# Two graph layers on one core: the second layer's adjacency tiles from a transposed input on GpSimd's queue, in place of a stored copy turned by DMA

## Chip, core and metric

The kernel runs on one core of one Trainium2 chip. The metric is the device time of one execution in microseconds (us), the median over the runs. Three runs of the kernel before gave 2017.46, 2017.54 and 2022.37 us.

## What is computed

```python
def layer0(query, key, value, adj, Wq, bq, Wk, bk, Wv, bv, Wm, bm):
    q, k, v = query @ Wq.T + bq, key @ Wk.T + bk, value @ Wv.T + bv
    scores = (q @ k.T) / 4096 ** 0.5 * adj
    scores = where(abs(scores) < 1e-05, -1e9, scores)
    return softmax(scores) @ v @ Wm.T + bm
def layer1(features, adj, W, b):
    return relu(adj @ features @ W.T + b)
x = layernorm(x + layer0(x, key, value, adj, ...))
x = layernorm(x + layer1(x, adj, W, b))
```

x, key and value are 4096 x 512 and adj is 4096 x 4096, all float32 in device memory; adj holds zeros and ones. The output is 4096 x 512.

## The kernel before

**Layer 0.** Rows are taken in 32 tiles of 128 (NT = 32). The keys are cut in two halves, and each half is a pass over all 32 row tiles, so there are 64 units, numbered 0 to 63. For a unit TensorE makes the scores (`scores`, line 934), VectorE masks them with a half row block of the adjacency (`adjh`, two buffers, loaded by GpSimd's queue in `load_adj`, line 771, with float32 turned into bf16 on the way), ScalarE makes exponentials, both split the probabilities into an fp16 high and low part (`Phl`), SyncE's queue turns these by DMA transposes (`turn_prob`: `PT<-Phl`, lines 423 and 426), and TensorE weighs the values with them (`weigh`, line 954). In the second pass the merged result is split (`Uhl`), turned (`turn_merged`, lines 552 and 555), multiplied by the joined weights (`project`, line 975) and normalised; this is a row tile of x1. It is split, turned (`turn_x1`, lines 539 and 542, into the single buffer `x1T`, only after the tile before it has been multiplied) and multiplied by W (`rows_product`, line 989): a tile of Y. Each operand is held as high and low part, and a product of two is 48 or 12 matmuls of 512 columns. In the second pass TensorE goes round: scores of unit g, rows_product, weigh of unit g - 1, project of unit g - 2.

**Layer 1.** With W applied first, what is left is adj @ Y. `AT[h][k]` are four SBUF buffers of 1 MB, each one row tile of the adjacency turned. Output tiles come in pairs p = 0 to 15, tile p and tile p + 16. Pairs 0 and 1 are plain products (`aggregate`, line 1061, 64 matmuls a tile). Pairs 2 to 15 (`seven`, line 1094) use seven products of 16 matmuls in place of eight blocks: VectorE makes four sums of adjacency blocks for the next pair (`adj_sum`, line 2153) and combines the results (`pair`, lines 2160 and 2165), adds bias and x1, and normalises (lines 2108 to 2124). For the last pair `last_pair` (line 2214) does it in halves of 256 columns.

**Where the adjacency tiles come from.** In every unit SyncE's queue stores the half row block that GpSimd's queue has loaded (`store_adj`, `adj_bf<-adjh`, line 410) as bf16 in device memory. Pairs 0 and 1 are turned from there in quarters (`adj_part`, line 560) between the other work of SyncE's queue at the end of layer 0: six quarters before the last unit's probabilities, two after x1 tile 29, four after the last merged tile, and four at the end. From pair 2 on whole tiles are turned (`adj_tile`, line 566), as soon as six of the seven products of pair p - 2 are made. Each queue works in its written order, and a wait holds everything written behind it.

**The order at the end of layer 0.** Y is in memory by now but for its last tiles. GpSimd's queue loads it in seven groups of four tiles, 1 MB each (`load_y`, line 794): groups 0 and 1 early, 4, 5 and 6 once the last probabilities are turned, 2 and 3 once x1 tile 30 is turned; then the signed sums (`load_sums`, 5.5 MB in all). TensorE's order is:

```
weigh(63); rows_product(28); project(62)
aggregate(0,0, m 0-8); rows_product(29); aggregate(0,0, 16-20); project(63)
aggregate(0,0, 20-28); aggregate(0,1, 0-8); rows_product(30)
aggregate(0,1, 16-28); aggregate(1,0, 0-8); rows_product(31)
aggregate(0,k, 8-16), the last four m of both, the rest of pair 1; seven() for pairs 2 to 15
```

## Time and profile before

| | us |
|---|---|
| median of three runs | 2017.54 |
| the profiled execution | 2020.34 |
| its span, first to last instruction | 2018.7 |
| TensorE busy | 1999.7 |
| VectorE busy | 1461.4 |
| ScalarE busy | 687.0 |

The stages by TensorE's work: weights, queries and keys to about 120 us, the first pass to 825, the second to 1598, the change to layer 1 to 1672, the fourteen pairs of seven products to 2010, and then the last tile's end. A row of a timeline gives start and duration in us, engine, line, operation and count; in brackets stands the idle time before it and what ended that. Matmuls overlap: a row's duration is longer than its pace, which is 216 ns a matmul everywhere (10.36 us for 48). PEclk is 1.00 where TensorE is granted its full 2.4 GHz. Times to landing are counted from the issue of a DMA to its semaphore.

### The profile page before, as it was taken

How to read it: one execution, taken by the hardware profiler on the slowest of the kernel's cores; microseconds unless marked ns; L12 is line 12 of the kernel's file. 1: busy time of each engine (PE TensorE's matmuls, PEld its weight loads, DVE VectorE, ACT ScalarE, POOL GpSimd, SP SyncE). 2: the span in 40 equal slices, each digit the busy share in tenths (PEclk: the TensorE clock that was granted, in tenths of full speed). 3: DMA queues.
4: the chain of work that ended last, by engine and by line, in shares of the span. 5: the costliest groups of instructions: out<-in, count | busy, mean ns of one | idle time of the engine just before them, and what ended most of it. 6: DMA issues, size and time to landing. Idle time of an engine off the chain costs nothing.

```text
span 2018.7 us, 29119 instructions
## 1 busy us (share of the span) xinstructions
PE 1999.7 (99%) x9243; PEld 915.3 (45%) x9243; DVE 1461.4 (72%) x3380; ACT 687.0 (34%) x853; POOL 95.3 (5%) x141
## 2 busy tenths in 40 slices
PE   8999999999999999999999999999999999999998
PEld 5444444444444444444444444444444444444443
DVE  7875666656666666777777777788888668788887
ACT  6853433334343443433333333344343210000000
POOL 5000000000000000000000000000000000000000
PEclk9999999999999999999999999999999999999999
DMA  7667777667777777777666667777777996555551
GB/s 284 242 172 171 189 186 201 155 155 161 188 171 181 179 170 215 180 165 167 166 166 162 162 165 165 165 166 182 180 184 206 223 277 141 125 130 137 130 134 62
DMA packets 564919, 351.22 MB, mean 174 GB/s; under 512 B 482176, under 2 KB 486272, under 8 KB 562944
## 3 DMA queue, kind: packets, MB, share of 16 engines
q1 hardware_dynamic: 547072, 279.26, 54.9%
q0 software_dynamic: 17792, 71.31, 15.4%
q8 instruction: 25, 0.41, 0.1%
q14 instruction: 30, 0.25, 0.0%
HBM read 176.95 MB, written 88.60 MB: 132 GB/s over the span
## 4 chain that ended last, share of the span: by engine, by line
PE 98%; SPq 1%; DVE 1%; DMA 0%; issue 0%; ACT 0%; DVEq 0%
PE ps L954 33%; PE ps L934 33%; PE ps L1094 17%; PE ps L905 4%; PE ps L989 4%; PE ps L975 4%; PE ps L1061 2%; SPq L560 1%; PE ps L853 0%; PE ps L848 0%; DMA x1T<-x1hl 0%; DMA wb<-in_Wk 0%; PE ps L835 0%; PE ps L866 0%; DVE weighed L1480 0%
## 5 line engine op out<-in xcount | busy, mean ns | idle before, releaser
L954 PE MATMUL ps<-V,PT 128*128 128x512 f16 x3072 | 673.3, 379 | 1.0 <-issue 1.0
L934 PE MATMUL ps<-KT,thl 128*128 128x512 f16 x3072 | 673.2, 379 | 0.0
L954 PEld LDWEIGHTS ps<-V,PT 128*128 128x128 f16 x3072 | 300.5, 98 | 363.7 <-issue 2.0
L934 PEld LDWEIGHTS ps<-KT,thl 128*128 128x128 f16 x3072 | 300.6, 98 | 362.2
L1718 DVE SCALAR_TENSOR_TENSOR prob<-ps,c_now,adjh 128x512 f32<-128x512 f32 x256 | 191.8, 750 | 262.3 <-PE ps L934 261.2
L1273 ACT ACTIVATE small<-prob 128x512 f32<-128x512 f32 x256 | 161.1, 630 | 619.3 <-DVE prob L1718 334.0
L1747 DVE SCALAR_TENSOR_TENSOR Phl<-prob,Phl 128x2048 f16<-128x2048 f32 x64 | 146.6, 2291 | 73.8 <-ACT Phl L1286 73.6
L1731 DVE CUSTOM_DVE_ANT_0 prob<-prob,small 128x512 f32<-128x512 f32 x256 | 174.4, 683 | 0.0
L1278 ACT ACTIVATE prob<-prob,nbias,inv 128x2048 f32<-128x2048 f32 x64 | 134.0, 2094 | 99.6 <-DVE nbias L1740 99.6
L1724 DVE TENSOR_SCALAR small<-small,eps_s,neg_s 128x512 f32<-128x512 f32 x256 | 138.9, 542 | 21.0 <-ACT small L1273 21.0
L1286 ACT ACTIVATE Phl<-prob 128x2048 f16<-128x2048 f32 x64 | 122.3, 1910 | 7.1
L1449 ACT ACTIVATE p<-ps 128x512 f32<-128x512 f32 x14 | 8.4, 597 | 323.5 <-PE ps L1094 323.5
L776 POOL DMA_DIRECT2D adjh<-in_adj x64 | 35.8, 559 | 1365.6 <-DMA adj_bf<-adjh 725.1
L1094 PE MATMUL ps<-Y,AT 128*128 128x512 f16 x448 | 99.0, 379 | 0.0
L975 PE MATMUL ps<-Wvm,UT 128*128 128x512 f16 x384 | 88.1, 379 | 2.5 <-DMA UT<-Uhl 2.5
L989 PE MATMUL ps<-W1T,x1T 128*128 128x512 f16 x384 | 88.1, 379 | 0.1
L905 PE MATMUL ps<-xT,Aq 128*128 128x512 f16 x384 | 84.5, 379 | 0.4 <-DVE xT L1558 0.4
L1094 PE MATMUL ps<-Ta,S 128*128 128x512 f16 x336 | 79.4, 379 | 0.0
L1094 PE MATMUL ps<-Tb,S 128*128 128x512 f16 x336 | 79.4, 379 | 0.0
L1094 PEld LDWEIGHTS ps<-Y,AT 128*128 128x128 bf16 x448 | 43.8, 98 | 52.9
L975 PEld LDWEIGHTS ps<-Wvm,UT 128*128 128x128 f16 x384 | 37.5, 98 | 48.0 <-DMA UT<-Uhl 3.0
L989 PEld LDWEIGHTS ps<-W1T,x1T 128*128 128x128 f16 x384 | 37.5, 98 | 45.7 <-DMA x1T<-x1hl 0.6
(208 smaller groups left out, 1695.1 us busy)
## 6 DMA issues: line engine op xcount, KB each, us to landing
adjh<-in_adj POOLq DMA_DIRECT2D x64, 512.0 KB, 5.4
adj_bf<-adjh SPq DMA_DIRECT2D x64, 512.0 KB, 4.6
t_in<-t_dram SPq DMA_DIRECT2D x64, 256.0 KB, 3.2
x_in<-in_x SPq DMA_DIRECT2D x64, 256.0 KB, 4.5
xraw<-in_x_t SPq DMA_DIRECT2D x8, 1024.0 KB, 8.6
t_dram<-tq POOLq DMA_DIRECT2D x8, 1024.0 KB, 5.8
o_dram<-z_out SPq DMA_DIRECT2D x32, 256.0 KB, 2.8
o_in<-o_dram SPq DMA_DIRECT2D x32, 256.0 KB, 4.6
```

Source lines behind the costliest of these rows:

```text
L905: last = nc.tensor.matmul(ps[:, BT + e, :], Aq[:, m, k, e * P:(e + 1) * P], xT[:, b, s, k, :], start=(n == 0), stop=(n == 3 * KD - 1))
L934: last = nc.tensor.matmul(ps[:, BS + c, :], thl[:, b, s, k * P:(k + 1) * P], KT[:, m, k, c * C:(c + 1) * C], start=(n == 0), stop=(n == 3 ...
L954: last = nc.tensor.matmul(ps[:, BU + b, :], PT[:, b, s, m, :], V[:, v, m, :], start=(m == 0 and q == 0), stop=(m == MT - 1 and q == 2))
L975: last = nc.tensor.matmul(ps[:, BZ, :], UT[:, b, s, k, :], Wvm[:, m, k, :], start=(n == 0), stop=(n == 3 * KD - 1))
L989: last = nc.tensor.matmul(ps[:, BY, :].rearrange("p (o n) -> p o n", n=P), x1T[:, s, k, :], W1T[:, m, :, k, :], start=(q == 0), stop=(q == ...
L1094: last = nc.tensor.matmul(ps[:, bank, :].rearrange("p (s d) -> p s d", s=2), left(m), right(m), start=(m == 0), stop=(m == NP - 1))
L1273: nc.scalar.activation(small[:, c % 2, :], prob[:, b, c * C:(c + 1) * C], ACT.Abs).then_inc(s_abs, 1)
L1278: nc.scalar.activation(prob[:, b, :], prob[:, b, :], ACT.Exp, bias=nbias[:, b:b + 1], scale=inv[:, half:half + 1], accum_out=rsum[:, b:b + ...
L1718: nc.vector.scalar_tensor_tensor(out=prob[:, b, c * C:(c + 1) * C], in0=ps[:, BS + c, :], scalar=c_now[:, b:b + 1], in1=adjh[:, b, c * C:( ...
L1724: nc.vector.tensor_scalar(small[:, c % 2, :], small[:, c % 2, :], eps_s[:, half:half + 1], neg_s[:, half:half + 1], ALU.is_lt, ALU.mult).t ...
L1731: nc.vector.tensor_tensor_reduce(out=prob[:, b, c * C:(c + 1) * C], in0=prob[:, b, c * C:(c + 1) * C], in1=small[:, c % 2, :], scale=1.0, ...
L1747: nc.vector.scalar_tensor_tensor(out=Phl[:, b, LO, :], in0=prob[:, b, :], scalar=P_SCALE, in1=Phl[:, b, HI, :], op0=ALU.mult, op1=ALU.subt ...
```

## The change

The host hands over a second form of the adjacency, `adj_t`, float32, in which each row tile is already laid out turned: `adj_t[t, p, m, n]` is `adj[128 t + n, 128 m + p]`. GpSimd's queue loads a tile of it straight into its buffer, with float32 turned into bf16 on the way (`load_tile`, 2 MB read and 1 MB written). `store_adj`, `adj_part`, `adj_tile` and the copy `adj_bf` are gone; `turned_used` keeps the wait that `store_adj` had. Tiles 0 and 16 are loaded in the middle of the second pass, so their buffers have moved to where the first half's keys were, and eight tiles of Y have moved to the probabilities' place (`Yfront`, read through `y_tiles`); groups 0 and 1 of Y are loaded later for that. TensorE's order at the end of layer 0 differs, and the last pair's end is written anew: the upper tile's right half is scaled in two steps straight from PSUM, and the lower tile's last step is on ScalarE. In the diff, waits for `16 * PARTS` quarters, which become waits for 16, and places where `Y[:, n]` became `y_tiles(n, 1)` are left out, as are declarations.

```diff
@@ -165,13 +165,15 @@
         with ExitStack() as second:
-            Y = sb(second, "Y", [P, NT, 2, D], fp16)
+            AT00 = sb(second, "AT00", [P, NT, P], bf16)
+            AT01 = sb(second, "AT01", [P, NT, P], bf16)
+            Y = sb(second, "Y", [P, NT - FRONT, 2, D], fp16)
             Ta = sb(second, "Ta", [P, PT2, 4, 2, H], fp16)
-            AT00 = sb(second, "AT00", [P, NT, P], bf16)
+            Yfront = sb(second, "Yfront", [P, FRONT, 2, D], fp16)
             AT10 = sb(second, "AT10", [P, NT, P], bf16)
-            AT01 = sb(second, "AT01", [P, NT, P], bf16)
             AT11 = sb(second, "AT11", [P, NT, P], bf16)
             with ExitStack() as signs:
                 Yr = sb(signs, "Yr", [P, 2, 2, D], fp32)
...
@@ -186,6 +188,9 @@
             Tb = sb(second, "Tb", [P, PT2, 4, 2, H], fp16)
             S34 = sb(second, "S34", [P, 2, HALF], bf16)
         AT = ((AT00, AT01), (AT10, AT11))
+        def y_tiles(n, count):
+            return Yfront[:, n:n + count, :, :] if n < FRONT else Y[:, n - FRONT:n - FRONT + count, :, :]
...
@@ -363,6 +368,10 @@
         def place(p, k):
             return 2 * p + (k if p < PLAIN else 1 - k)
+        LOWER_READY = (ROOT_STEPS + 3) * 2 * (NP - 1) + 8 + 2 + 2 * ROOT_STEPS - 2 + 1
...
@@ -403,12 +412,9 @@
                     wait(sp, s_z, n - 1)
                     load_x(n, b)
-                def store_adj(g, n, b, j, half):
+                def turned_used(g):
                     wait(sp, o_mm, g - 1)
-                    sp.wait_ge(adj_in[b], 16 * (j + 1))
-                    sp.dma_start(adj_bf[bass.ds(n * P, P), half * HALF:(half + 1) * HALF], adjh[:, b, :])\
-                      .then_inc(ab_st[b], 16)
...
@@ -455,9 +461,11 @@
                     nb, nj = 1 - b, j + b
                     load_t(g + 2, (g + 2) % NT if isinstance(g, int) else g + 2)
+                    if not isinstance(g, int):
+                        sp.to_reg(g - 1)
                     wait(sp, s_c, g)
+                    turned_used(g)
                     load_x(g + 1, nb)
-                    store_adj(g, g, b, j, 0)
                     if chunk is not None:
                         load_chunk(2 * chunk + b, b, chunk)
                     turn_prob(g, b)
...
@@ -554,17 +562,6 @@
                     sp.wait_ge(u_lo, g - NT + 1)
                     sp.dma_start_transpose(UT[:, b, LO, :, :], Uhl[:, LO, :]).then_inc(ul_in[b], 16)
-                def adj_part(p, k, part):
-                    t, w = p + NP * k, N // PARTS
-                    sp.dma_start_transpose(AT[p][k][:, part * (NT // PARTS):(part + 1) * (NT // PARTS), :],
-                                           adj_bf[t * P:(t + 1) * P, part * w:(part + 1) * w]).then_inc(at_in[p][k], 16)
-                def adj_tile(p, k):
-                    t = p + NP * k
-                    sp.dma_start_transpose(AT[p % 2][k][:, :, :], adj_bf[t * P:(t + 1) * P, :]).then_inc(at_in[p % 2][k], 16)
...
@@ -592,18 +591,6 @@
                         if isinstance(n, int) and n == NT - NP + TC:
                             sp.wait_ge(yf_st, 16 * NP)
                         load_copy(n - NP - TC, b)
-                    if isinstance(n, int) and n == NT - 1:
-                        for k in range(2):
-                            sp.wait_ge(ab_st[k], 16 * (NT // 2 + NP // 2 + 1))
-                        sp.wait_ge(p_lo, g)
-                        for part in range(PARTS):
-                            adj_part(0, 0, part)
-                        sp.wait_ge(ph_in[0], 16 * NT)
-                        sp.wait_ge(pl_in[0], 16 * NT)
-                        for part in range(2):
-                            adj_part(0, 1, part)
                     turn_prob(g, b)
...
@@ -654,22 +641,13 @@
                 last = 2 * NT - 1
                 turn_x1(NT - 3)
                 store_x1(NT - 3, 1)
-                for part in range(2, PARTS):
-                    adj_part(0, 1, part)
                 turn_merged(last, 1)
-                sp.wait_ge(p_lo, 2 * NT)
-                for part in range(PARTS):
-                    adj_part(1, 0, part)
                 turn_x1(NT - 2)
                 store_x1(NT - 2, 0)
                 sp.wait_ge(y_st, 16 * (NT - TC))
                 sp.dma_start(b1_rep[:, :], b1.rearrange("(a n) -> a n", a=1).to_broadcast([P, D])).then_inc(s_bm, 16)
                 turn_x1(NT - 1)
                 store_x1(NT - 1, 1)
-                sp.wait_ge(ph_in[1], 16 * NT)
-                sp.wait_ge(pl_in[1], 16 * NT)
-                for part in range(PARTS):
-                    adj_part(1, 1, part)
...
@@ -679,28 +657,20 @@
                     sp.dma_start(zf[:, k, :], x1_dram[t * P:(t + 1) * P, :]).then_inc(zf_in[k], 16)
                 for b in range(2):
-                    sp.wait_ge(ab_st[b], 16 * NT)
                     sp.wait_ge(o_st[b], 16 * NT)
                 for k in range(2):
                     load_row(0, k)
-                for p in range(NP):
-                    if p + 2 < NP:
-                        q = p - PLAIN
-                        if q < 0:
-                            sp.wait_ge(f_mm, 2 * (p + 1))
-                        else:
-                            sp.wait_ge(s_prod, 7 * q + 6)
-                            sp.wait_ge(s_comb, 4 * (q + 1))
-                        for k in range(2):
-                            adj_tile(p + 2, k)
-                    if p + 1 < NP:
-                        for k in range(2):
-                            load_row(p + 1, k)
+                for p in range(1, NP):
+                    for k in range(2):
+                        load_row(p, k)
                 for k in (1, 0):
                     t = NP - 1 + NP * k
-                    sp.wait_ge(f_res, place(NP - 1, k) + 1)
+                    if k == 1:
+                        sp.wait_ge(s_lower, 1)
+                    else:
+                        sp.wait_ge(f_res, place(NP - 1, k))
                     sp.dma_start(out[t * P:(t + 1) * P, :], y[:, k, :]).then_inc(last_st, 16)
                 sp.wait_ge(last_st, 32)
                 for k in range(2):
...
@@ -772,7 +742,6 @@
                     if not isinstance(g, int) or g >= 2:
                         pool.wait_ge(s_adj, MC * (g - 1))
-                        pool.wait_ge(ab_st[b], 8 * (g - b))
                     pool.dma_start(adjh[:, b, :], adj[bass.ds(n * P, P), half * HALF:(half + 1) * HALF])\
                         .then_inc(adj_in[b], 16)
...
@@ -785,13 +754,28 @@
                 with pool.Fori(1, NT // 2) as i:
                     for b in range(2):
                         load_adj(2 * i + b, b, 2 * i + b, 0)
-                with pool.Fori(0, NT // 2) as i:
+                def load_tile(p, k):
+                    t = p + NP * k
+                    pool.dma_start(AT[p % 2][k][:, :, :], adj_t[t, :, :, :]).then_inc(at_in[p % 2][k], 16)
+                SECOND = (NP + TC) // 2
+                with pool.Fori(0, SECOND) as i:
                     for b in range(2):
                         load_adj(2 * i + b, b, NT + 2 * i + b, 1)
+                pool.wait_ge(w_turned, 32)
+                for k in range(2):
+                    load_tile(0, k)
+                    load_adj(2 * SECOND + k, k, NT + 2 * SECOND + k, 1)
+                with pool.Fori(SECOND + 1, NT // 2) as i:
+                    for b in range(2):
+                        load_adj(2 * i + b, b, NT + 2 * i + b, 1)
                 def load_y(c):
                     pool.wait_ge(y_st, 16 * TC * (c + 1))
-                    pool.dma_start(Y[:, c * TC:(c + 1) * TC, :, :],
+                    pool.dma_start(y_tiles(c * TC, TC),
                                    y_dram[c * TC:(c + 1) * TC, :, :, :].rearrange("t p s d -> p t s d")).then_inc(y_ld[c][0], 16)
...
-                pool.wait_ge(w_turned, 32)
-                for c in (0, 1):
-                    load_y(c)
+                pool.wait_ge(p_lo, 2 * NT - 1)
+                load_y(0)
                 pool.wait_ge(pl_in[1], 16 * NT)
+                load_y(1)
                 for c in (4, 5, 6):
                     load_y(c)
+                pool.wait_ge(ph_in[0], 16 * NT)
+                pool.wait_ge(pl_in[0], 16 * NT)
+                load_tile(1, 0)
                 pool.wait_ge(ts_st, 16 * EARLY)
                 pool.wait_ge(x1t_in, 32 * (NT - 1))
                 for c in (2, 3):
                     load_y(c)
+                pool.wait_ge(ph_in[1], 16 * NT)
+                load_tile(1, 1)
                 pool.wait_ge(x1t_in, 32 * NT)
                 for c in range(2):
                     load_sums(c, Ta[:, 4 * c:4 * c + 4, :, :, :])
                 pool.wait_ge(y_mm, NT)
                 load_sums(2, Tb[:, 0:EARLY - 8, :, :, :])
-                for k in range(2):
-                    store(0, k)
-                for p in range(1, NP - 1):
+                for p in range(NP - 1):
+                    if p + 2 < NP:
+                        q = p - PLAIN
+                        if q < 0:
+                            pool.wait_ge(f_mm, 2 * (p + 1))
+                        else:
+                            pool.wait_ge(s_prod, 7 * q + 6)
+                            pool.wait_ge(s_comb, 4 * (q + 1))
+                        for k in range(2):
+                            load_tile(p + 2, k)
                     for k in range(2) if p < PLAIN else (1, 0):
                         store(p, k)
...
@@ -1058,26 +1057,26 @@
                             elif m % TC == 0:
                                 pe.wait_ge(*y_ld[m // TC])
                         for s in (HI, LO):
...
+                pe.wait_ge(s_adj, MC * 2 * NT)
+                aggregate(0, 0, 0, 4)
                 project(2 * NT - 2, 0, NT - 1)
-                pe.wait_ge(s_adj, MC * 2 * NT)
-                aggregate(0, 0, 0, 8)
+                aggregate(0, 0, 4, 8)
                 rows_product(NT - 3)
-                aggregate(0, 0, NP, NP + 4)
+                aggregate(0, 1, 0, 8)
                 project(2 * NT - 1, 1, NT - 1)
-                aggregate(0, 0, NP + 4, NT - TC)
-                aggregate(0, 1, 0, 8)
+                aggregate(0, 0, NP, NT - TC)
                 rows_product(NT - 2)
                 aggregate(0, 1, NP, NT - TC)
+                rows_product(NT - 1)
                 aggregate(1, 0, 0, 8)
-                rows_product(NT - 1)
                 for k in range(2):
                     aggregate(0, k, 8, NP)
...
@@ -1452,6 +1451,9 @@
                     copy_first_product(q)
                 with act.Fori(2, NP - PLAIN) as q:
                     copy_first_product(q)
+                act.wait_ge(f_step, LOWER_READY)
+                nc.scalar.activation(y[:, 1, :], y[:, 1, :], ACT.Identity, bias=ra2[:, 1:2], scale=rstd2[:, 1:2]).then_inc(s_lower, 1)
             @block.vector
...
@@ -2256,33 +2266,42 @@
                     taken(q, 3, u2[:, :], p1[:, :], ps[:, 3, :], ALU.add)
                     dve.wait_ge(c_step, 11 * q + 3)
                     taken(q, 4, u5[:, :], u2[:, :], ps[:, 2, :], ALU.add)
+                    dve.wait_ge(c_step, 11 * q + 4)
+                    nc.vector.tensor_tensor(cs[:, 0, H:D], u5[:, 0:H], u5[:, H:D], ALU.add).then_inc(c_step, 1)
                     dve.wait_ge(s_prod, 7 * q + 5)
-                    dve.wait_ge(c_step, 11 * q + 4)
-                    taken(q, 5, csum[:, 1, :], u5[:, :], ps[:, 6, :], ALU.add)
-                    together(q, 5, 1, 1, 1)
-                    taken(q, 7, u3[:, :], u2[:, :], ps[:, 6, :], ALU.add)
-                    half(1, 1, bst2, 6)
+                    taken(q, 6, csum[:, 1, :], u5[:, :], ps[:, 6, :], ALU.add)
+                    together(q, 6, 1, 1, 1)
+                    taken(q, 8, u3[:, :], u2[:, :], ps[:, 6, :], ALU.add)
+                    half(1, 1, bst2, 7)
+                    scaled(0, 1, cs[:, 0, H:D], b1_rep[:, H:D])
                     dve.wait_ge(s_prod, 7 * q + 6)
-                    dve.wait_ge(c_step, 11 * q + 7)
-                    taken(q, 8, csum[:, 0, :], u3[:, :], ps[:, 5, :], ALU.subtract)
-                    together(q, 8, 0, 1, 0)
-                    half(1, 0, bst2, 9)
+                    dve.wait_ge(c_step, 11 * q + 8)
+                    taken(q, 9, csum[:, 0, :], u3[:, :], ps[:, 5, :], ALU.subtract)
+                    together(q, 9, 0, 1, 0)
+                    half(1, 0, bst2, 10)
                     begin(1, bst2)
                     for step in range(2):
                         root_step(1, step, 0)
                     dve.wait_ge(s_prod, 7 * q + 7)
-                    taken(q, 10, csum[:, 1, :], u5[:, :], ps[:, 4, :], ALU.add)
-                    together(q, 10, 1, 0, 1)
-                    half(0, 1, bst, 11)
+                    for s in range(2):
+                        dve.wait_ge(f_out, done[0])
+                        scaled(0, 1, ps[:, 4, s * H:(s + 1) * H], y[:, 0, H:D])
+                    deviation(0, 1, bst)
                     begin(0, bst)
                     for step in range(ROOT_STEPS - 2):
                         root_step(1, step + 2, 1)
                         root_step(0, step, 1)
                     dve.wait_ge(f_step, steps[0] - 1)
-                    finish(1)
-                    for step in range(ROOT_STEPS - 2, ROOT_STEPS):
-                        root_step(0, step, 0)
+                    nc.vector.scalar_tensor_tensor(out=ra2[:, 1:2], in0=mv2[:, 1, 0:1], scalar=-1.0, in1=rstd2[:, 1:2],
+                                                   op0=ALU.mult, op1=ALU.mult).then_inc(f_step, 1)
+                    steps[0] += 1
+                    assert steps[0] == LOWER_READY
+                    root_step(0, ROOT_STEPS - 2, 1)
+                    root_step(0, ROOT_STEPS - 1, 0)
                     dve.wait_ge(f_step, steps[0])
                     finish(0)
...
@@ -2301,7 +2320,7 @@
     x, key = inputs["x"], inputs["L0_gnn_key"]
     half = key.shape[0] // 2
-    laid_out = [("x", x), ("x_t", blocks(x, 512)), ("adj", inputs["adj"]),
+    laid_out = [("x", x), ("x_t", blocks(x, 512)), ("adj", inputs["adj"]), ("adj_t", blocks(inputs["adj"], 128)),
                 ("key_t0", blocks(key[:half], 512)), ("key_t1", blocks(key[half:], 128))]
     for name in ("value", "Wq", "Wk", "Wv"):
         laid_out.append((name, inputs["L0_gnn_" + name]))
```

## Rows read from the trace of the kernel before

**Rows 1.** Page, part 1: busy us and share of the span.

```profile
PE 1999.7 (99%) x9243; PEld 915.3 (45%) x9243; DVE 1461.4 (72%) x3380; ACT 687.0 (34%) x853; POOL 95.3 (5%) x141
```

**Rows 2.** Windows: stretch, us, busy of each engine, PEclk, DMA share, GB/s.

```profile
200.00:400.00 200.00, 200.00 (x929) 90.78 (x928) 133.26 (x266) 76.45 (x88) 5.33 (x10) 1.00 0.76 183
...
1840.00:1864.00 24.00, 24.00 (x113) 10.88 (x112) 19.53 (x44) 0.60 (x1) 1.08 (x2) 1.00 0.52 131
```

**Rows 3.** Timeline of TensorE at the end of layer 0.

```profile
1587.67 10.52 PE L954 MATMUL ps<-V,PT 128*128 128x512 f16 x48 [0.51 <-issue]
...
1603.28 2.75 PE L975 MATMUL ps<-Wvm,UT 128*128 128x512 f16 x12 [2.50 <-DMA UT<-Uhl]
...
1616.22 7.07 PE L1061 MATMUL ps<-Y,AT 128*128 128x512 f16 x32
1623.41 2.76 PE L989 MATMUL ps<-W1T,x1T 128*128 128x512 f16 x12
...
1634.64 2.75 PE L989 MATMUL ps<-W1T,x1T 128*128 128x512 f16 x12
```

**Rows 4.** Timeline of SyncE's queue in the same stretch.

```profile
1569.63 9.14 SPq L560 DMA_TRANSPOSE AT<-adj_bf  x6
...
1583.27 1.35 SPq L426 DMA_TRANSPOSE PT<-Phl  x1
...
1590.98 2.05 SPq L552 DMA_TRANSPOSE UT<-Uhl  x1
...
1626.26 1.26 SPq L539 DMA_TRANSPOSE x1T<-x1hl  x1
```

**Rows 5.** DMA from 1588 to 1600: queue, packets, MB, share; then issues, us to landing.

```profile
q0 software_dynamic: 506, 1.98, 61.6%
q1 hardware_dynamic: 1209, 0.97, 41.9%
...
UT<-Uhl SPq DMA_TRANSPOSE x2, 10.9
```

**Rows 6.** DMA from 1626 to 1630; no other queue has a row there.

```profile
q0 software_dynamic: 351, 1.37, 92.1%
...
x1T<-x1hl SPq DMA_TRANSPOSE x2, 6.5
```

**Rows 7.** DMA from 1636 to 1650.

```profile
q0 software_dynamic: 397, 5.53, 94.7%
q1 hardware_dynamic: 809, 0.20, 8.2%
```

**Rows 8.** DMA from 1314 to 1322: one load of adjh.

```profile
q0 software_dynamic: 144, 0.52, 41.3%
```

**Rows 9.** DMA view of the whole run: issues, median us to landing.

```profile
UT<-Uhl SPq DMA_TRANSPOSE x64, 2.5
```

**Rows 10.** Timelines of VectorE around x1 tile 30, and of POOL.

```profile
1610.95 0.69 DVE L1851 SCALAR_TENSOR_TENSOR x1hl<-z_out,x1hl 128x512 f16<-128x512 f32 x1 [0.70 <-ACT x1hl L1338]
...
1587.97 1.49 POOL L794 DMA_DIRECT2D Y<-y_dram  x2 [63.80 <-DMA PT<-Phl]
```

**Rows 11.** Timelines of SyncE's queue and VectorE in one pair of seven products.

```profile
1837.72 9.41 SPq L566 DMA_TRANSPOSE AT<-adj_bf  x2
...
1853.34 1.22 DVE L2153 TENSOR_TENSOR S<-AT 128x2048 bf16<-128x2048 bf16 x1
```

**Rows 12.** Timeline of VectorE at the end.

```profile
2007.00 0.69 DVE L2160 TENSOR_TENSOR csum<-u,ps 128x512 f32<-128x512 f32 x1 [0.37 <-PE ps L1094]
...
2010.39 0.69 DVE L2160 TENSOR_TENSOR csum<-u,ps 128x512 f32<-128x512 f32 x1
...
2011.58 0.48 DVE L2223 SCALAR_TENSOR_TENSOR y<-cs,inv_y,b_rep 128x256 f32<-128x256 f32 x1
2012.17 0.42 DVE L2228 SCALAR_TENSOR_TENSOR y<-y,zf 128x256 f32<-128x256 f32 x1
...
2014.76 0.54 DVE L2247 TENSOR_SCALAR y<-y,mv,rstd 128x512 f32<-128x512 f32 x1
```

47 lines of the change are left out of this document (27 added, 20 removed).

## The prediction

> **What bounds the kernel now.** I read the page's busy times first, then the windows, then the timelines of TensorE and of SyncE's queue at the end of layer 0, the DMA view by short stretches, and the end. TensorE is busy for 1999.7 of 2018.7 us [rows 1], and in the passes without a break and at the full clock [rows 2]. The change leaves every matmul in place, so only TensorE's idle time can move. Of that some 7 us lie before 100 us, where nothing changes. Three gaps lie at the end of layer 0: 0.51 us before weigh(63), 2.50 us before project(62), which waits for the turned merged tile, and 0.3 us before rows_product(30) [rows 3] (its row starts at 1623.41, while 32 matmuls of 216 ns from 1616.22 end at 1623.13). The rest is the end after the last matmul, from 2010.39 on [rows 12].
>
> The sum is made on the profiled execution, 2020.34 us, which is 2.8 us above the median of the runs, 2017.54. I take the same difference off the median.
>
> **The passes: 0.** 64 stores of the half row block leave SyncE's queue, and DMA traffic falls. TensorE waits for none of it [rows 2], so this buys nothing. `turned_used` keeps the wait. The first two tiles are loaded in the second pass on GpSimd's queue, each ahead of one load of adjh. One load of adjh keeps the 16 DMA engines for 41.3% of 8 us = 3.3 us [rows 8]. A tile is twice the bytes, so 6.6 us. The load of adjh behind it is issued when unit g - 2 is masked, some 40 us ahead of its own masking, and the transposes of the unit have over 10 us to spare before TensorE wants them. Cost 0; if that cover were gone, 6.6 us twice.
>
> **The pairs of seven products: 0.** SyncE's two transposes took 9.4 us to issue, from 1837.72, and VectorE took the first sum from the tiles at 1853.34 [rows 11], 15.6 us later. After the change two loads of 6.6 us each and about 2 us to start and land make 15.2 us. VectorE is busy for 19.53 of 24 us [rows 2], so a few us more are made up within the pair, and TensorE wants that sum only some 17 us after it is made (it serves the third product of the next pair). The two zf loads and the two stores of a pair (1 MB) fit beside 13.2 us in 24.2. Two stores now stand behind two loads on GpSimd's queue; they are issued 7 and 14 us later, when their data are made, and nobody waits for them for some 10 us. Cost 0.
>
> **The end of layer 0.** This is where the change decides. SyncE's queue loses sixteen quarter transposes; six ran just before the last probabilities were turned [rows 4]. GpSimd's queue gains: group 1 of Y moves behind the last probabilities, next to groups 4, 5 and 6, and a tile follows at once. Before, groups 4 and 5 stood there alone, issued at 1587.97 [rows 10]. So after 1588 there are 4 MB of Y and a tile of 6.6 us in one unbroken row on that queue, where there were 2 MB, a pause, and 1 MB.
>
> *What such a load does to a transpose.* A transpose of a merged or x1 tile lands 2.5 us after issue in calm [rows 9]. With two groups of Y under way it took 10.9 [rows 5]. From 1626 to 1630, with x1T issued at 1626.26 [rows 4], GpSimd's queue moved 351 packets and the hardware queue none, and x1T landed after 6.5 us, about 1.3 us after the last packets of the load [rows 6]. From 1636 to 1650 the hardware queue moved 809 packets in 14 us, 58 a us, beside 5.53 MB [rows 7]. So the transposes advance hardly or slowly as long as GpSimd's queue has work.
>
> By the Trainium skill ("DMA: Bandwidth & Descriptors", Queues, rings and completion order) an engine takes turns between its queues, packet by packet. This trace agrees from 1636 to 1650 at most and not from 1626 to 1630, where a queue that had been issued to got no turn.
>
> *The gap of 0.51.* It ends as the last low transpose, issued at 1583.27 [rows 4], lands 4.3 us later. Without the quarters ahead of the pair [rows 4] I put its issue where VectorE has made its data, at about 1582.8, and its landing at 1587.1. **-0.5.**
>
> *project(62).* TensorE now comes to it at 1587.16 + 10.36 + 2.59 + 8 x 0.216 = 1601.8. SyncE issues the merged tile's two transposes at about 1589.0 and 1590.3, 2 us earlier than before, as nothing stands in its way; GpSimd's data start at about 1589.5. Y drains at 1.37 MB in 4 us = 0.34 MB a us [rows 6]: 4 MB take 11.8 us, and with the tile the queue is empty at 1607.9. If the transposes slip in ahead they land by 1601.8 and TensorE waits for nothing; if they wait for all of it, at 1609.4, a gap of 7.6. At 58 packets a us [rows 7] their some 1,000 packets take 17.7 us, to 1608. Part of the first gets through before the load is at full strength, so I take 1606, a gap of 4.2 where there were 2.5: **+1.7**. rows_product(29) is then reached at 1606 + 2.6 + 1.7 = 1610.3, and x1T of tile 29, issued at 1600.2, lands at about 1609.4 with the queue: no further gap.
>
> *project(63), rows_product(30).* SyncE's queue has no quarters now between the x1 and merged transposes. x1T of tile 30 needs 5.8 us from the end of project(62) (1605.86 to 1611.64 [rows 10]), and TensorE has 11.2 us of other work between rows_product(29) and (30). **-0.3**, the small gap.
>
> *rows_product(31).* It now comes 5.2 us after rows_product(30), where it came 8.6 us after it [rows 3]. Its transposes can't be issued before rows_product(30) ends, because `x1T` is single. GpSimd's queue begins groups 2 and 3 and then tile (1,1) when x1T of tile 30 has landed, and I put that 8 us after rows_product(29) starts. Then come 2 us to start, 2 MB at 0.34 = 5.9, and 6.6 for the tile: free at 22.5, x1T landed at 23.8, while TensorE comes at 21.6. Gap 2.2. At the 0.395 MB a us of [rows 7], with the tile's 2 MB read at that pace too, it is 0. I take the middle: **+1.1**.
>
> Tiles for pairs 2 and 3 are issued as pairs 0 and 1 end, behind 5.5 MB of signed sums; at 0.395 these are over by about 1655, and two tiles by about 1668, before 1671.9 when pair 2 starts. **0.** The sums of VectorE start with rows_product(31) and have 3.4 us more to spare than before.
>
> **The end.** Before, 2010.39 to 2012.17 goes for a sum of 512 columns, a join and a scaling [rows 12]. Two scalings of 256 columns, 0.59 from one to the next as in the last two of these rows, take 1.2: -0.6. One more such scaling stands before the last product, in a stretch with 0.37 us to spare: +0.15. The lower tile's last step, 0.54 between the root steps, goes to ScalarE for one of 0.2: -0.3. Its store goes ahead of the last one as before. Together **-0.8**, between -0.9 and 0.
>
> **Sum:** -0.5 + 1.7 - 0.3 + 1.1 - 0.8 = +1.2, so 2021.5 for such an execution and **2018.7** as the median.
>
> **Rivals.**
> *A, the queue of loads holds TensorE up (slower).* The transposes for project(62) and for rows_product(31) wait for all that is ahead on GpSimd's queue. At 0.34 MB a us the gaps are 7.6 and 2.2: -0.5 + 5.1 - 0.3 + 2.2 - 0.8 = +5.7. At the pace of 1.98 MB in some 9 us [rows 5], 0.22, Y takes 18.2 us, the merged tile lands at 1615.8, gap 14.0, and the second is some 5: +14.9. The middle, **2027**. It is past the bound of slower once the merged tile lands after 1609.9. For it: rows 5 and 6. Against it: the two transposes are issued 2 us sooner.
> *B, the transposes slip through.* No gap is left: -3.3 - 0.8 = -4.1, **2013.4**. By the skill's turns the merged tile gets every second packet; at the 58 a us that the trace shows beside a load that is 1608, not in time, so the rule alone doesn't make this case. It needs the head start or shorter loads.
> *C, the pairs become bound by their loads.* Were two tiles to take over 24.2 us instead of 15.2, each of 14 pairs would stretch; at 27 us that is +39, **2057**. Against it: 3.3 us for half a tile [rows 8].
> *D, the copy's removal frees TensorE in the passes.* Against it: no gap there [rows 2].
>
> **How the numbers follow.** Forecast 0.42, A 0.25, B 0.25, C 0.02, and 0.06 for a gain past every term (D, or a run-to-run difference). A measurement of this kernel can tell about 0.3%, 6 us. The forecast and B are within it: same 0.67. Slower is A and C, 0.27; faster 0.06. The range takes in B whole and A to its middle: 2013.0 to 2027.5.
>
> **What would show it.** Right: TensorE's timeline has no gap before weigh(63), one of 2 to 6 us before project(62) ended by UT<-Uhl, none before rows_product(30), a short one before rows_product(31); VectorE takes a pair's first sum within 3 us of the time before, and TensorE has no gap from pair 2 on; the span ends 7.5 us after the last product instead of 8.3. Wrong: transposes with landings of 2.5 us amid the loads (B), hardware packets near none until 1610 or later (A), or VectorE waiting for AT in every pair (C).

## The result, and the profile after

Nine executions of the changed kernel have a median of 2027.95 us (2026.45 to 2036.92), nine of the kernel before 2018.74 us. The ratio is 1.0054, with a 95% interval of 1.0044 to 1.0064. So the change is slower, by 9.2 us in the medians, where 2018.7 us was forecast and the range ended at 2027.5. That is the place where rival A stood (2027). Six of the nine took 2026.45 to 2029.01 us and three 2033.31 to 2036.92.

The profiled execution took 2026.45 us (span 2024.8) and is the fastest of the nine. Beside that of before (2020.34, span 2018.7) it is 6.1 us longer. First the page's busy times, after:

```profile
PE 2000.0 (99%) x9243; PEld 914.9 (45%) x9243; DVE 1461.3 (72%) x3381; ACT 687.6 (34%) x854; POOL 116.3 (6%) x173
```

Against [rows 1] TensorE has the same work, 9243 matmuls, and GpSimd has 32 instructions more. What differs is idle time of TensorE and one stretch at half its clock, worked out below. Windows of the kernel after (stretch, us, busy of each engine, PEclk, DMA share, GB/s): a piece of the first pass, six pieces at the end of layer 0, and the pairs of seven products.

```profile
200.00:400.00 200.00, 200.00 (x928) 90.77 (x927) 133.77 (x268) 77.02 (x88) 5.40 (x10) 1.00 0.68 157
...
1599.00:1607.00 8.00, 6.44 (x30) 2.57 (x27) 3.53 (x7) 1.11 (x2) 0.26 (x1) 1.00 1.12 292
1607.00:1609.00 2.00, 0.00 (x0) 0.00 (x0) 1.68 (x10) 0.00 (x0) 0.00 (x0) 1.00 1.14 219
1609.00:1611.00 2.00, 0.00 (x0) 0.00 (x0) 0.45 (x1) 0.00 (x0) 0.00 (x0) 0.65 0.93 191
1611.00:1613.00 2.00, 0.00 (x0) 0.00 (x0) 0.00 (x0) 0.00 (x0) 0.00 (x0) 0.50 1.25 136
1613.00:1615.00 2.00, 1.55 (x4) 0.59 (x5) 0.69 (x1) 0.63 (x1) 0.00 (x0) 0.50 0.80 211
1615.00:1617.00 2.00, 2.00 (x7) 0.77 (x6) 0.00 (x0) 0.00 (x0) 0.00 (x0) 0.64 0.00 0
```

```profile
1672.00:1990.00 318.00, 318.00 (x1475) 144.16 (x1474) 256.42 (x560) 7.76 (x13) 29.08 (x53) 1.00 0.56 130
```

These pieces of the passes and of the pairs have no gap, and from 300 to 825 us TensorE is busy for 524.87 of 525 us; DMA traffic in the first pass fell from 183 [rows 2] to 157 GB/s and bought nothing. Between 1607 and 1613.45 us TensorE does nothing, and in that pause the granted clock falls to 0.50, the lower level of 1.2 GHz, and returns to 1.00 only after 1615.

TensorE's timeline after, the rows that answer to [rows 3]:

```profile
1586.13 10.52 PE L953 MATMUL ps<-V,PT 128*128 128x512 f16 x48 [0.32 <-issue]
...
1602.47 2.75 PE L974 MATMUL ps<-Wvm,UT 128*128 128x512 f16 x12 [1.51 <-DMA UT<-Uhl]
1605.06 1.89 PE L1060 MATMUL ps<-Yfront,AT 128*128 128x512 f16 x8
1613.45 4.23 PE L988 MATMUL ps<-W1T,x1T 128*128 128x512 f16 x12 [6.50 <-DMA x1T<-x1hl]
...
1620.97 2.75 PE L974 MATMUL ps<-Wvm,UT 128*128 128x512 f16 x12
...
1637.70 2.76 PE L988 MATMUL ps<-W1T,x1T 128*128 128x512 f16 x12 [1.03 <-DMA x1T<-x1hl]
```

A row of TensorE names what a wait ended with; `rows_product` multiplies a turned tile of x1 (`x1T`), `project` a turned merged tile (`UT`). The large gap, 6.50 us, stands before rows_product(29), where I forecast none, and the wait is for x1T of tile 29. The 28 matmuls from 1613.45 to 1620.97 take 7.52 us, where 28 x 0.216 is 6.05: the low clock costs 1.47 us more. Against the kernel before: -0.19 before weigh(63), -0.99 before project(62), +6.50 and +1.47 here, -0.28 before rows_product(30), +1.03 before rows_product(31). That is +7.5.

To compare executions without the scatter of the kernel's beginning I measure a **stretch**: from where TensorE is done before weigh(63) (its start less its gap) to the start of the last product's 16 matmuls. Before it is 2006.74 - 1587.16 = 419.58, after 2013.26 - 1585.81 = 427.45, so +7.87: the gaps and the clock, to within 0.3 us.

Now GpSimd's and SyncE's queues after:

```profile
1586.43 0.76 POOL L778 DMA_DIRECT2D Yfront<-y_dram  x1 [29.27 <-DMA PT<-Phl]
1587.18 1.49 POOL L778 DMA_DIRECT2D Y<-y_dram  x2
1597.96 0.75 POOL L778 DMA_DIRECT2D Y<-y_dram  x1 [9.29 <-DMA y_dram<-Yst]
1598.70 0.57 POOL L761 DMA_DIRECT2D AT<-in_adj_t  x1
...
1623.51 0.57 POOL L761 DMA_DIRECT2D AT<-in_adj_t  x1
```

```profile
1591.63 3.69 SPq L563 DMA_TRANSPOSE UT<-Uhl  x1
...
1599.33 1.21 SPq L547 DMA_TRANSPOSE x1T<-x1hl  x1
1600.63 1.21 SPq L550 DMA_TRANSPOSE x1T<-x1hl  x1
1601.89 0.57 SPq L538 DMA_DIRECT2D x_dram<-z_out  x1
1602.70 7.08 SPq L560 DMA_TRANSPOSE UT<-Uhl  x1
```

Groups 1, 4 and 5 of Y go out together, but group 6 waits 9.29 us for the store of its tiles and goes out at 1597.96, with the tile (1,0) behind it at 1598.70. In this pause the merged tile's transposes get through, and project(62) starts at 1602.47. Group 6's own data come late: from 1601 to 1603 GpSimd's queue moved 5 packets, from 1603 to 1606 282. The two transposes of x1 tile 29 are issued 0.6 and 1.9 us after the tile's load; the first lands after 13.7 us, the second at about 1613.3. One more transpose behind them even takes 7.08 us to be issued.

The DMA queues from 1606 to 1608 and from 1608 to 1610 (queue, packets, MB, share of 16 engines):

```profile
q0 software_dynamic: 45, 0.36, 94.4%
q1 hardware_dynamic: 45, 0.01, 7.3%
...
q0 software_dynamic: 48, 0.39, 93.6%
q1 hardware_dynamic: 49, 0.01, 4.7%
```

GpSimd's queue moved 45 packets and SyncE's 45, then 48 and 49. So here the two queues advance one for one, but a packet of the tile's load is 8 KB and one of a transpose 0.25 KB. It isn't so wherever a load and a transpose meet. The transposes of x1 tile 31 were issued at 1631.58 and 1632.87, beside tile (1,1), and from 1632 to 1634 the hardware queue has no row at all:

```profile
q0 software_dynamic: 53, 0.43, 104.7%
```

From 1612 to 1614, with the load of tile (1,0) over, the hardware queue moved 1073 packets:

```profile
q1 hardware_dynamic: 1073, 0.48, 96.5%
```

**The end.** VectorE's timeline, the rows that answer to [rows 12], then ScalarE's step for the lower tile and the two stores on SyncE's queue:

```profile
2016.92 1.00 DVE L2223 SCALAR_TENSOR_TENSOR y<-ps,inv_y,y 128x256 f32<-128x256 f32 x2
2018.03 0.43 DVE L2238 SCALAR_TENSOR_TENSOR y<-y,zf 128x256 f32<-128x256 f32 x1
...
2021.19 0.55 DVE L2257 TENSOR_SCALAR y<-y,mv,rstd 128x512 f32<-128x512 f32 x1
...
2020.81 0.81 ACT L1456 ACTIVATE y<-y,ra,rstd 128x512 f32<-128x512 f32 x1 [23.92 <-DVE ra L2298]
...
2021.65 0.82 SPq L674 DMA_DIRECT2D out<-y  x2
```

From the last product's 16 matmuls to the end of the span it is 11.54 us, where it was 11.96: -0.42.

### The profile page after: what moved, and what is told of

It reads as the page before. It is cut to its first block, busy times and chain, and to the rows that moved or that the text cites. A ratio compares the mean times of both kernels' runs of the same rounds, so it can differ in the third digit from the quotient of the medians.

```text
span 2024.8 us, 28869 instructions
## 1 busy us (share of the span) xinstructions
PE 2000.0 (99%) x9243; PEld 914.9 (45%) x9243; DVE 1461.3 (72%) x3381; ACT 687.6 (34%) x854; POOL 116.3 (6%) x173
## 4 chain that ended last, share of the span: by engine, by line
PE 98%; DMA 1%; DVE 1%; SPq 0%; ACT 0%; issue 0%; DVEq 0%
PE ps L953 33%; PE ps L933 33%; PE ps L1093 17%; PE ps L988 4%; PE ps L904 4%; PE ps L974 4%; PE ps L1060 2%; DMA x1T<-x1hl 1%; PE ps L852 0%; PE ps L847 0%; DVE weighed L1482 0%; DVE Aq L1601 0%; DMA wb<-in_Wk 0%; PE ps L834 0%; DVE mcol L1588 0%; DVE xT L1560 0%
## 5 line engine op out<-in xcount | busy, mean ns | idle before, releaser
L1093 PE MATMUL ps<-Y,AT 128*128 128x512 f16 x336 | 74.8, 379 | 0.0
L904 PEld LDWEIGHTS ps<-xT,Aq 128*128 128x128 f16 x384 | 37.5, 98 | 45.6 <-DVE xT L1560 1.4
```

The source lines that it names most:

```text
L904: last = nc.tensor.matmul(ps[:, BT + e, :], Aq[:, m, k, e * P:(e + 1) * P], xT[:, b, s, k, :], start=(n == 0), stop=(n == 3 * KD - 1))
L1093: last = nc.tensor.matmul(ps[:, bank, :].rearrange("p (s d) -> p s d", s=2), left(m), right(m), start=(m == 0), stop=(m == NP - 1))
```

## The experiments

Each kernel was timed in three rounds beside the kernel before on the same chip (the last one in five). The ratio and its interval are those given for these runs side by side; it isn't the quotient of the two medians and can differ from it by 0.2%. Gaps and stretch are from the profiled execution; the first two gaps stand before weigh(63) and project(62), where nothing else is named, and "half clock" means that the group behind a gap took over 4 us for 12 matmuls instead of 2.75, or over 12.9 for 48 instead of 10.52.

| kernel | median, before | ratio, 95% interval | stretch | gaps of TensorE at the end of layer 0, us |
|---|---|---|---|---|
| before | | | 419.58 | 0.51; project(62) 2.50; rows_product(30) 0.28 |
| after | 2027.95, 2018.74 | 1.0054 (1.0044 to 1.0064) | 427.45 | 0.32; 1.51; rows_product(29) 6.50, half clock; (31) 1.03 |
| e1 | 2026.67, 2018.81 | 1.0030 (1.0014 to 1.0045) | 426.22 | 0.23; 2.09; (29) 1.82; (31) 3.76, half clock |
| e2 | 2026.32, 2018.81 | 1.0025 (1.0011 to 1.0039) | 427.30 | 0.21; 2.22, half clock; (31) 3.88, half clock |
| e3 | 2023.90, 2018.81 | 1.0015 (1.0000 to 1.0030) | 422.95 | 0.63; 0.66; (29) 3.82, half clock |
| e4 | 2027.96, 2018.81 | 1.0025 (1.0000 to 1.0050) | 428.03 | 0.20; 3.82, half clock; (29) 3.20, half clock |
| e5 | 2018.40, 2018.78 | 0.9996 (0.9986 to 1.0005) | 418.35 | 0.64; 1.07; (30) 0.18 |
| e6 | 2024.61, 2018.78 | 1.0044 (1.0028 to 1.0060) | 422.43 | weigh(63) 2.83; 0.34; (29) 1.24; (31) 1.38 |
| e7 | 2027.67, 2018.78 | 1.0040 (1.0025 to 1.0055) | 425.42 | weigh(63) 3.21, half clock; 3.00 |
| e8 | 2026.36, 2018.78 | 1.0030 (1.0020 to 1.0039) | 424.95 | weigh(63) 4.13, half clock; project(63) 2.14 |
| e9 | 2018.08, 2018.78 | 0.9995 (0.9985 to 1.0005) | 417.07 | weigh(63) 0.55; project(63) 0.26 |
| e10 | 2020.25, 2018.78 | 1.0012 (1.0002 to 1.0023) | 419.47 | 0.23; 1.52; (29) 1.26 |
| e11 | 2021.05, 2019.08 | 1.0005 (0.9991 to 1.0020) | 421.65 | 0.71; 0.54; (29) 1.93; (30) 1.38; (31) 0.29 |
| e12 | 2017.98, 2019.08 | 0.9995 (0.9985 to 1.0005) | 417.04 | 0.59; project(63) 0.16 |

### e1 and e2: the first tile, then group 6 too, behind x1 tile 29

```diff
# e1: the change, tile (1,0) later
                 pool.wait_ge(pl_in[0], 16 * NT)
+                pool.wait_ge(x1t_in, 32 * (NT - 2))
                 load_tile(1, 0)
# e2: the change, group 6 and the tile later
-                for c in (4, 5, 6):
+                for c in (4, 5):
                     load_y(c)
...
+                pool.wait_ge(x1t_in, 32 * (NT - 2))
+                load_y(6)
                 load_tile(1, 0)
```

> The kernel after, but GpSimd's queue loads tile (1,0) only when x1T of tile 29 has landed. Theory T (the 2 MB tile load with its 8 KB packets holds up the transposes of x1T 29, which take turns with it): the wait before rows_product(29) falls from 6.5 us to 2 or 3 us (group 6 of Y is still ahead), and TensorE's clock does not fall there (1.5 us more); the time falls by 4 to 6 us, to some 2023. Theory G (the four groups of Y alone do it): the wait stays above 5 us and the time falls by less than 1.5 us. Theory O (only TensorE's new order exposes waits): no change.

> As before it, but group 6 of Y too is loaded only when x1T of tile 29 has landed, so that nothing of GpSimd's queue is beside it after about 1600. Theories T and G: no wait before rows_product(29); 6 to 8 us below the kernel after, some 2021. The wait for UT before project(62), 1.5 us, stays, since groups 1, 4 and 5 are where they were; a later wait for group 6 or for tile (1,0) may come up, under 2 us. Theory O: no change.

The gap before rows_product(29) falls from 6.50 to 1.82 without the tile, and to nothing without group 6 as well. This ties the gap to these two loads. The times that I had expected, some 2023 and 2021, were missed: x1T of tile 31 is now late in place of x1T of tile 29. TensorE's timeline of e1:

```profile
1609.86 2.76 PE L989 MATMUL ps<-W1T,x1T 128*128 128x512 f16 x12 [1.82 <-DMA x1T<-x1hl]
1635.37 4.23 PE L989 MATMUL ps<-W1T,x1T 128*128 128x512 f16 x12 [3.76 <-DMA x1T<-x1hl]
```

The load, moved by 12 us from 1598.70 to 1610.40, runs beside the transposes of x1 tile 30, which now land after 6.7 and 5.8 us, where they took 2.4 in the kernel after. TensorE doesn't wait there, but groups 2 and 3 and tile (1,1) wait for that landing (1620.39), and the transposes of x1 tile 31, issued at 1626.52 beside them, land after 8.3 and 7.5 us. The stretch is only 1.2 us shorter in e1 and 0.2 in e2; as e5 will show, that is no more than two executions of the same work can differ.

### e3: the kernel before with one load more

```diff
                 for c in (4, 5, 6):
                     load_y(c)
+                pool.wait_ge(s_adj, MC * 2 * NT)
+                pool.dma_start(adjh[:, :, :].rearrange("p b n -> p (b n)"), adj[0:P, :]).then_inc(extra, 16)
```

The load reads 2 MB of float32 and writes 1 MB into a buffer that nobody reads any more, so it is extra work at the place of the tile; all else is as before.

> The kernel before with one more load of 2 MB float32 to 1 MB bf16 (rows 0 to 127 of the adjacency, into adjh, which is free then) behind group 6 on GpSimd's queue, where the kernel after loads tile (1,0). Theory T: x1T of tile 29 lands some 4 us later and a wait of 3 to 5 us appears before rows_product(29), where there was none, with the clock falling for part of it if it is long; the time rises by 4 to 6 us over before. Theories G and O: the time rises by less than 1 us.

```profile
1609.93 4.15 PE L992 MATMUL ps<-W1T,x1T 128*128 128x512 f16 x12 [3.82 <-DMA x1T<-x1hl]
```

As theory T expected, one load is enough to bring a gap of 3.82 us before rows_product(29), half clock included, in a kernel that has none there; the stretch is 3.4 us longer and the median 5.1 us. The ratio of the runs side by side says less, 1.0015, and its interval begins at 1.0000, so what shows the effect is the gap, not the time. One of the ten executions took 7142.53 us and is not in the ratio; nothing here explains it. The DMA queues of e3 from 1606 to 1608 show the turns again, 49 packets against 49:

```profile
q0 software_dynamic: 49, 0.40, 95.5%
q1 hardware_dynamic: 49, 0.01, 4.7%
```

### e4: the change in the old order of TensorE

```diff
# the change, with TensorE's order at the end of layer 0 as before
-                aggregate(0, 0, 0, 4)
-                aggregate(0, 0, 4, 8)
+                aggregate(0, 0, 0, 8)
...
-                aggregate(0, 0, NP, NT - TC)
+                aggregate(0, 0, NP + 4, NT - TC)
+                aggregate(0, 1, 0, 8)
```

> The kernel after with TensorE's order of the kernel before at the end of layer 0. Theory O: the waits go, and the time falls to within 2 us of before. Theories T and G: the wait before project(62) is 3 to 4 us (it comes 1.7 us sooner), that before rows_product(29) 4 to 6 us (it comes 0 to 1.7 us later in the order), and none before rows_product(31), which comes 3.4 us later; the time is within 2 us of the kernel after.

Its median is that of the change, 2027.96 against 2027.95, and its stretch 428.03 against 427.45. The gap before rows_product(31) is gone, the one before rows_product(29) is smaller and the one before project(62) larger, each of these two with half clock (I had expected 4 to 6 us there, it is 3.20). The new order is not what costs the time, so theory O falls. Whether it saves a little isn't decided: the ratio is 1.0025, below that of the change, with an interval that reaches to 1.0050.

### e5: only the new end

```diff
# the kernel before with the new last_pair, ScalarE's step and the two stores' waits
-                    sp.wait_ge(f_res, place(NP - 1, k) + 1)
+                    if k == 1:
+                        sp.wait_ge(s_lower, 1)
+                    else:
+                        sp.wait_ge(f_res, place(NP - 1, k))
```

> The kernel before with the new end of the last pair alone (two scalings from PSUM, the lower tile's last step on ScalarE). Every theory: the span from TensorE's last matmul to the end falls from 8.3 to 7.5 or 7.9 us, the time by 0.4 to 0.8 us, which is under what the runs can tell; the stretch before is unchanged.

From the last product's 16 matmuls (2005.20) to the span's end (2016.7) it is 11.5 us again, 0.46 less than before, and the medians differ by 0.4. The interval includes no difference. That execution's stretch, in which its instructions are the same as before, is 1.2 us shorter than before's (its project(62) waited 1.07 us instead of 2.50): so much do two executions of the same work differ here, though I had expected the same.

### e6 to e8: the first tile early

```diff
# e6: the change, the tile behind group 0, in place of behind group 6
                 load_y(0)
+                pool.wait_ge(ph_in[0], 16 * NT)
+                pool.wait_ge(pl_in[0], 16 * NT)
+                load_tile(1, 0)
# e7: e6, and tile (1,1) behind the last transpose of x1
                 pool.wait_ge(x1t_in, 32 * NT)
+                load_tile(1, 1)
# e8: e7, and group 4 behind UT of tile 30, groups 5 and 6 behind x1T of tile 29
```

> The kernel after, with tile (1,0) loaded right behind group 0 of Y, once the last even unit's probabilities are turned, some 35 us sooner. Theory T (what counts is which transposes a load of GpSimd's queue runs beside): the wait before rows_product(29) falls from 6.5 us to 0 to 2 us; that before rows_product(31) rises to some 3 us, as groups 2 and 3 and tile (1,1) follow x1T of tile 30 as before while TensorE comes there sooner; the time falls by 4 to 6 us against the kernel after. Rival V (the total of bytes in the stretch counts, not their place): the time falls as much as for e1, 1 to 2 us.

> As e6, and tile (1,1) is loaded only when x1T of tile 31 has landed. Theory T: the wait before rows_product(31) falls to 0 to 2 us (groups 2 and 3 are still beside it); what is left are 1.5 to 2 us before project(62) and 0 to 2 before rows_product(29); the time is within 2 us of the kernel before, at about 2018. Rival V: no change against e6.

> As e7, and group 4 waits until the merged tile 62 is turned, groups 5 and 6 until x1T of tile 29 has landed. Theory T: no wait over 1 us is left at the end of layer 0; the time is 2 to 4 us below the kernel before, 2014.5 to 2017. Rival V: the groups come late, aggregate waits for them, and the time is that of e7 or above.

In all three the gap has moved ahead of weigh(63). The tile, issued at 1569.99 in e6, keeps the load of the x tile (`x_in`) waiting; VectorE's normalisation waits for that, and the last low transpose of the probabilities goes out at 1586.90, where it went out at 1581.72 after the change. VectorE and SyncE's queue in e6:

```profile
1580.51 0.69 DVE L1798 TENSOR_TENSOR x_in<-x_in,bias_o 128x512 f32<-128x512 f32 x1 [2.84 <-DMA x_in<-in_x]
```

```profile
1581.79 1.92 SPq L429 DMA_TRANSPOSE PT<-Phl  x1
1586.90 1.84 SPq L432 DMA_TRANSPOSE PT<-Phl  x1
```

In e7 and e8 half clock follows the pause (13.46 and 12.92 us for 48 matmuls). The gap before rows_product(29) fell as theory T expected (1.24 us, then none), but T had not seen the new one, and its times were missed: e6 is 3.3 us below the change, where 4 to 6 were expected, and e7 and e8 are at 2027.67 and 2026.36, where 2018 and 2014.5 to 2017 were. e6's nine executions reach from 2022.85 to 2033.59 us, so its ratio (1.0044) and its one profile, near the low end, tell different things. None of the three places tried among the last transposes (behind group 0, behind group 6, behind x1 tile 29) was free for 2 MB of reading. e7 and e8 also show that with tile (1,1) behind the last transpose rows_product(31) waits for nothing. The waits of 3.00 us before project(62) in e7 and of 2.14 before project(63) in e8 were not followed up.

### e9, e10 and e12: both tiles behind the last transpose

```diff
# e10: the change, both tiles late, so pair 1 is all behind pair 0
-                load_tile(1, 0)
...
                 pool.wait_ge(x1t_in, 32 * NT)
+                load_tile(1, 0)
+                load_tile(1, 1)
...
-                aggregate(1, 0, 0, 8)
-                aggregate(1, 0, 8, NT)
+                aggregate(1, 0, 0, NT)
# e9 and e12: e10, and group 4 behind UT of tile 30, groups 5 and 6 behind x1T of tile 29
```

> As e8, but tile (1,0) too is loaded only when x1T of tile 31 has landed, and TensorE does all of pair 1 behind pair 0 (the first eight steps of (1,0) no longer stand behind rows_product(31)). Nothing but one or two groups of Y is ever beside a transpose. Theory T: no wait over 1 us at the end of layer 0, and tile (1,0), issued some 13 us before TensorE wants it, lands in time; 2014.5 to 2017, 2 to 4 us below the kernel before. If the waits stay (over 5 us in all), what holds the transposes is not the load that is beside them, and theory T falls.

> The kernel after with both tiles of pair 1 behind x1T of tile 31 and TensorE's order as in e9, the groups of Y as in after (1, 4, 5 and 6 in a row). Theory T: waits of 1.5 us before project(62) and about 2 before rows_product(29), as in e1 (group 6), none before rows_product(31) (groups 2 and 3 alone are beside it, as in the kernel before, though TensorE comes 3.4 us sooner: 0 to 2 us): 2017 to 2020. It tells the share of the tiles from that of the groups.

With the tiles away the loss is nearly gone: e10 has 2020.25, a ratio of 1.0012 in place of 1.0054. With the groups between the transposes too (e9) it is gone: 2018.08, 0.9995. By the medians, of the 9.9 us from the change to e9 the two tiles, with pair 1 behind pair 0, are 7.7 and the groups of Y 2.2; by the stretches 8.0 and 2.4. The move of pair 1 alone was not run. The gaps came as expected; the time of e9 did not reach 2014.5 to 2017.

e9's profiled execution is the slowest of its ten (2023.35), though its stretch is among the shortest. It lost its time at the start of the kernel, in a gap of TensorE that no other profile has:

```profile
46.36 0.48 PE L841 MATMUL ps<-ident,gsq 128*128 128x128 f32 x1 [5.88 <-DVE gsq L1508]
```

A run again, in more rounds:

> The kernel of e9 again in more rounds: the change, with tiles (1,0) and (1,1) loaded behind the last transpose of x1, groups 4 to 6 between the transposes, and pair 1 of tiles all behind pair 0. Theory (the late tiles take away the whole loss, and the shorter end and the absent last gaps give 1 to 3 us): 2015.5 to 2018.0 us, which is 0.7 to 3 below the kernel before and about 10 below the change. Rival (what is gained at the end of the first layer is inside the scatter of the runs): 2018 to 2020, no difference from the kernel before.

2017.98 against 2019.08 of the kernel before, ratio 0.9995, interval 0.9985 to 1.0005. It beats the change by some 10 us. Against the kernel before the median stands at the upper edge of what the theory expected, but the interval includes no difference, so the rival isn't excluded and a gain isn't shown. TensorE and GpSimd's queue in e12:

```profile
1606.67 2.75 PE L991 MATMUL ps<-W1T,x1T 128*128 128x512 f16 x12
1613.04 2.75 PE L977 MATMUL ps<-Wvm,UT 128*128 128x512 f16 x12 [0.16 <-issue]
1620.81 2.75 PE L991 MATMUL ps<-W1T,x1T 128*128 128x512 f16 x12
1628.58 2.75 PE L991 MATMUL ps<-W1T,x1T 128*128 128x512 f16 x12
```

```profile
1597.71 0.75 POOL L778 DMA_DIRECT2D Y<-y_dram  x1 [8.97 <-issue]
1605.43 1.49 POOL L778 DMA_DIRECT2D Y<-y_dram  x2 [6.97 <-DMA x1T<-x1hl]
...
1627.67 1.09 POOL L761 DMA_DIRECT2D AT<-in_adj_t  x2 [9.18 <-DMA x1T<-x1hl]
```

Each load now begins when a transpose has landed, and no row of the three x1 tiles has a bracket. Beside the groups of Y the transposes are still slow: from 1610 to 1613, with x1T of tile 30 issued at 1610.06, GpSimd's queue moved 285 packets and the hardware queue 33, and the two landed after 5.9 and 5.1 us. TensorE came later than that. The profiled executions differ by 3.0 us (2017.31 and 2020.34), the medians only by 1.1; after e5 I put a good part of that to the executions and not to the kernels.

### e11: the extra load of e3 from the bf16 copy

```diff
# e3, with the source changed: 1 MB read in place of 2
-                pool.dma_start(adjh[:, :, :].rearrange("p b n -> p (b n)"), adj[0:P, :]).then_inc(extra, 16)
+                pool.dma_start(adjh[:, :, :].rearrange("p b n -> p (b n)"), adj_bf[0:P, :]).then_inc(extra, 16)
```

> The kernel before with a load of one extra adjacency tile behind group 6 on GpSimd's queue, as in e3, but read from the bfloat16 copy in DRAM (1 MB read, 1 MB written) instead of the float32 input (2 MB read, 1 MB written). Theory (the transposes take turns with the load's packets, and what one turn costs is the bytes that are read for it): the gap before rows_product(29) falls from e3's 3.8 us to 0 to 1.5 us, its first group of 12 matmuls takes 2.75 us again, and the time is 0 to 1.5 us over the kernel before (e3: 3 to 5 over). Rival (only the number of packets counts, or the bytes written): the gap stays at 3 to 4.5 us with a group of 4.2 us behind it, and the time is 3 to 5 us over.

```profile
1609.16 2.76 PE L992 MATMUL ps<-W1T,x1T 128*128 128x512 f16 x12 [1.93 <-DMA x1T<-x1hl]
```

The gap is 1.93 us instead of 3.82, at the full clock, and the median 2.0 us above before instead of 5.1. Both lie between the two expectations, nearer to the one by bytes read. From 1606 to 1608, e11:

```profile
q1 hardware_dynamic: 580, 0.14, 101.2%
q0 software_dynamic: 50, 0.28, 34.8%
```

580 packets of the transposes got through where e3 had 49, because this load was almost over by then. From 1605 to 1606, with it under way, the two queues went one for one again, at twice e3's pace:

```profile
q0 software_dynamic: 46, 0.38, 93.9%
q1 hardware_dynamic: 46, 0.01, 5.2%
```

That is 46 packets of 8 KB in 1 us, where e3 moved 49 in 2 us with the engines as busy. With the same bytes written, the load from float32 keeps the engines for twice as long, as the bytes read would have it. So the float32 source, which the change brings in with `adj_t`, is a good part of what the load costs here: half of this gap and all of the clock's part. Not all: e11 has a gap of 1.38 us before rows_product(30) that e3 has not, and its stretch is still 2.1 us longer than before's, against 3.4 in e3.

## Why the prediction was wrong

**Passes, 0: right.** TensorE has 200.00 of 200 us in them after as before.

**Pairs of seven products, 0: right.** A tile in this stage lands after 10.5 us in the median. From the pair of loads issued at 1844.51 VectorE takes its first sum at 1859.87, 15.4 us later, without a wait; that this is near my 15.2 says nothing of the loads, which were over by about 1858. It waits for a tile once, for 6.3 us, and TensorE never (318.00 of 318). Rival C falls, and so does D.

**The gap of 0.51, -0.5:** it is 0.32. The transpose went out at 1581.72, but this execution is 1.35 us ahead of the one that I worked from, and in that one's times this is 1583.07, 0.3 us later than the 1582.8 that I had put. That 0.3 is the gap.

**project(62), +1.7: the sign was wrong, -1.0.** I took 4 MB of Y as one unbroken row of loads. Group 6 waits for a store of Y that SyncE issues at 1587.38 and that lands 10.1 us later, and so leaves a pause of some microseconds, as it did in the kernel before; I had its wait in the code and left it out of the sum. The hardware queue moved 1117 packets from 1598 to 1602, and UT landed for 1602.47, not 1606. The 2 us of head start for UT's transposes didn't come either: the issuing of that store took 2.11 us, and they went out at 1590.13 and 1591.63, in the times of the kernel before 0.5 us later than there. The wait is shorter because TensorE now does 8 matmuls of pair 0 (1.73 us) first; in the old order (e4) it is 3.82. The kernel's rows of before had the two issues apart (2 MB, a pause, 1 MB, as the prediction itself says), and only the tile closes ranks with group 6.

**The step that failed is the last sentence of that paragraph:** "x1T of tile 29, issued at 1600.2, lands at about 1609.4 with the queue: no further gap". The issue was right (1599.33 and 1600.63). The queue's end was not: I had it at 1607.9. Group 6's data came from 1603 to 1606, and the tile's only behind them, to about 1611. GpSimd's queue from 1606 to 1612, of which 7 packets came after 1611:

```profile
q0 software_dynamic: 129, 0.93, 76.5%
```

x1T landed at about 1613.3, while TensorE, which had not lost its 4.2 us at project(62), was there at 1606.95. This is +6.50. Had I kept group 6 at 1598, 2 us to start, its 3 us and the tile's 6.6 would have put the queue's end near 1610 and the gap at some 4 us by the prediction's own prices. What is left is group 6's start, 5 us after its issue, less the tile's shorter time (below); why group 6 was so late is open.

**The price of a tile, 6.6 us, was not what failed.** I took it as twice a load of `adjh` alone [rows 8]. The tile landed 14.1 us after its issue, but most of that it stood behind group 6: its own data took about 5 us, from 1606 to 1611, with the transposes beside it.

**The clock, +1.47: not foreseen.** Before has full clock in its windows, the one with its 2.50 us gap included, and I didn't ask what a gap of several microseconds brings with it. In the table half clock stands behind nine gaps, of 2.22 to 6.50 us, and behind others, of up to 3.00 us (e7), it doesn't; so the length of the gap alone doesn't tell.

**rows_product(30), -0.3: right**, no gap. **rows_product(31), +1.1: 1.03, but in part by luck.** The steps hold: GpSimd's queue began groups 2 and 3 8.6 us after rows_product(29) started, where I put 8, and x1T landed at 24.2, where I put 23.8. But with TensorE there at 21.6 that makes 2.6 us, not 1.1; the 1.47 us of half clock behind rows_product(29), which I had not foreseen, let TensorE come later and took most of the difference.

**The end, -0.8: it is -0.42.** The scaling takes 1.11 us from 2016.92 to 2018.03, where it took 1.78 [rows 12]: -0.67, as worked out. From there to the last step VectorE needs 3.16 us, where it needed 3.49: -0.33, as worked out. The last step before:

```profile
2015.66 0.55 DVE L2247 TENSOR_SCALAR y<-y,mv,rstd 128x512 f32<-128x512 f32 x1
```

But the span ends 3.61 us after that step starts, where it was 3.04. On ScalarE the lower tile's step takes 0.81 us and ends at 2021.62, only 0.12 us ahead of VectorE's last step (2021.74). Its store is issued at 2021.65 and the last one behind it, so the last one has to wait for that. The rows fit this, but no run separates it, and it need not be all of the 0.57 us. I had written "its store goes ahead of the last one as before"; it does, but with no room between. The +0.15 for one more scaling didn't show (3.66 us from the last product to the first scaling, where it was 3.65).

**Sum.** By gaps and clock +7.5, the end -0.4: +7.1, beside +1.2 forecast; the profiled execution shows +6.1, since it reached the stretch 1.4 us sooner. The median is 9.2 above that of before. The step from 6.1 to 9.2 is that the profile of before is 1.6 us above its median and that of after, the fastest of nine, 1.5 below its own. What the longer executions of the change did has no profile. That the start of the kernel scatters by itself is shown by e9, whose profiled execution lost 5.88 us there.

**Rival A** named the mechanism: the transposes wait for what is ahead on GpSimd's queue. Its place was wrong: it had the gap at project(62) and (31), and by luck the median was near. Its own sum was off as well: the middle of +5.7 and +14.9 is +10.3, so 2027.8 and not 2027. Its condition, the merged tile landing after 1609.9, was not met.

By the Trainium skill ("DMA: Bandwidth & Descriptors", Queues, rings and completion order) an engine takes turns between its queues packet by packet; I had said that this trace agrees at one place at most. Beside a casting load the rows agree in some stretches: 45 against 45, 48 against 49, 49 against 49. In others they don't: 53 against none from 1632 to 1634 here, 51 against none in e1 from 1614 to 1616, with the transposes of x1 tile 30 issued at 1612.71, and none in the kernel before [rows 6]. What decides between the two no run here tells. In both the transposes landed only when the load was over, so its length is what counts, and on that the runs speak: e3 and e11 show what it is made of.

## What to carry to other kernels

A copy that is taken off one DMA queue and put as a large load on another isn't free where TensorE waits for small transposes: ask of each large load which small transfer is issued behind it, and begin it only when the last of these has landed (e9: 10 us). Here a load that turns float32 into bf16 kept the engines by what it reads (24 packets of 8 KB a us in e3, 46 from bf16 in e11). And a gap of several microseconds can cost more than its length, as the clock falls behind it.

In a sum over a queue keep every wait in its place: one wait that splits a row of loads decided here which transpose was late.

## What the hardware showed that I had not expected

- Beside the casting load both queues moved the same number of packets in some stretches (45 and 45 in 2 us), 8 KB against 0.25 KB each; in others the transposes got none (53 to 0 in 2 us). A transpose that lands in 2.5 us in calm [rows 9] took 13.7.
- After TensorE had done nothing from 1606.95 on, the granted clock was still 1.00 up to 1609, 0.65 up to 1611 and 0.50 (1.2 GHz) from there to 1615; it was 0.64 up to 1617 and 1.00 after that. The 28 matmuls from 1613.45 lost 1.47 us by it. In e7 48 matmuls behind a gap of 3.21 us took 13.46 us instead of 10.52.
- With the two transposes of x1 tile 29 still under way beside the loads, the issue of the next transpose took 7.08 us on SyncE's queue, where those two took 1.21 each, and what is written behind it went out only at 1609.86.
- Group 6 of Y, issued at 1597.96, moved its first data at about 1603, where groups 4 and 5 before, issued at 1587.97, moved theirs within 3 us (65 packets from 1590 to 1592).
